# Attention in a graph network on one core: VectorE's maxima and sums interleaved, and two heads' value products moved

## What is computed

```python
q = (x @ Wq + bq).reshape(N, H, HEAD)      # N = 512, H = 8, HEAD = 64
k = (x @ Wk + bk).reshape(N, H, HEAD)
v = (x @ Wv + bv).reshape(N, H, HEAD)
scores = jnp.einsum('nhd,mhd->nhm', q, k) / np.sqrt(HEAD)
adj = jnp.zeros((N, N), jnp.float32).at[edge_index[0], edge_index[1]].set(1.0)
scores = jnp.where(adj[:, None, :] == 0, -1000000000.0, scores)
attn = jax.nn.softmax(scores, axis=1)
attn_out = jnp.einsum('nhm,mhd->nhd', attn, v).reshape(N, D_OUT)
attn_out = attn_out @ Wo + bo
```

## Time and profile before

| | us |
|---|---|
| median of 3 runs | 477.36 |
| lowest and highest run | 476.39, 477.62 |
| profiled execution, its own time | 475.42 |
| its span, first to last instruction | 473.3 |
| TensorE busy | 450.0 (95%) |
| VectorE busy | 315.1 (67%) |
| ScalarE busy | 190.5 (40%) |
| GpSimd busy | 165.7 (35%) |

### The profile page before, as it was taken

How to read it: one execution, slowest core, us unless ns; L and a number is a source line. 1 busy time by engine, 2 the same in 40 slices (tenths; PEclk the granted TensorE clock), 3 DMA queues, 4 the chain that set the end, 5 groups by cost and what they waited for, 6 DMA issues and landing times.

```text
span 473.3 us, 5934 instructions
## 1 busy us (share of the span) xinstructions
PE 450.0 (95%) x2096; PEld 327.8 (69%) x2096; DVE 315.1 (67%) x570; ACT 190.5 (40%) x265; POOL 165.7 (35%) x110
## 2 busy tenths in 40 slices
PE   7999999979899998799999999999999999999996
PEld 3456544434359886678778788888888888888765
DVE  5999868999997986958865935342262237133864
ACT  5898734555133421252632353044303342227230
POOL 4000221212233996266242444144444444344100
PEclk9999999999999999799999999999999999999999
DMA  8760000000031244004011222222220332020002
GB/s 276 190 258 1 1 2 0 24 0 0 1 111 46 89 152 156 6 16 182 3 26 64 90 89 90 89 89 112 89 90 13 117 149 77 24 89 1 0 1 89
DMA packets 22474, 34.34 MB, mean 73 GB/s; under 512 B 5680, under 2 KB 5936, under 8 KB 22448
## 3 DMA queue, kind: packets, MB, share of 16 engines
q1 hardware_dynamic: 22160, 33.85, 20.3%
q10 hardware_dynamic: 288, 0.13, 0.1%
HBM read 32.93 MB, written 1.05 MB: 72 GB/s over the span
## 4 chain that ended last, share of the span: by engine, by line
PE 70%; DVE 18%; issue 6%; ACT 2%; POOL 1%; DVEq 1%; DMA 1%; POOLq 0%
PE ps L1236 15%; PE ps L1238 15%; PE ps L1237 15%; PE ps L1298 4%; PE ps L1309 4%; PE ps L1265 3%; PE ps L1264 3%; DVE rsum L947 2%; PE ps L1386 2%; DVE stats L754 2%; PE ps L1291 2%; DVE e_sb L384 2%; DVE one_src L828 1%; PE ps L1249 1%; PE ps L1565 1%
## 5 line engine op out<-in xcount | busy, mean ns | idle before, releaser
L463 POOL TENSOR_TENSOR w_lo<-w_stage,w_hi 128x1024 fp32r<-128x1024 f32 x22 | 53.6, 2434 | 129.7 <-ACT w_hi L554 118.9
L554 ACT ACTIVATE w_hi<-w_stage 128x2048 fp32r<-128x2048 f32 x23 | 43.9, 1909 | 61.8 <-PE ps L1238 61.8
L464 POOL TENSOR_TENSOR w_lo<-w_stage,w_hi 128x1024 fp32r<-128x1024 f32 x22 | 57.3, 2604 | 0.0
L1236 PE MATMUL ps<-w_hi,hid_hi 128*128 128x512 f32 x128 | 49.9, 390 | 0.5 <-DVE hid_lo L1147 0.5
L1237 PE MATMUL ps<-w_lo,hid_hi 128*128 128x512 f32 x128 | 49.8, 389 | 0.0
L1238 PE MATMUL ps<-w_hi,hid_lo 128*128 128x512 f32 x128 | 49.8, 389 | 0.0
L1236 PE MATMUL ps<-T_hi,w_hi 128*128 128x512 f32 (+1 forms) x112 | 41.0, 366 | 0.4 <-POOL w_lo L464 0.4
L1237 PE MATMUL ps<-T_lo,w_hi 128*128 128x512 f32 (+1 forms) x112 | 40.2, 359 | 0.0
L1238 PE MATMUL ps<-T_hi,w_lo 128*128 128x512 f32 (+1 forms) x112 | 40.2, 359 | 0.0
L1145 DVE TENSOR_SCALAR tmp<-ps,bl 128x512 f32<-128x512 f32 x16 | 12.0, 749 | 39.9 <-ACT hid_hi L705 39.9
L828 DVE TENSOR_SCALAR one_src<-iota_n,edge_m,edge_w 128x256 f16 x128 | 34.1, 334 | 0.4 <-POOL edge_w L500 0.4
(11 more groups left out here) (216 smaller groups left out, 998.2 us busy)
## 6 DMA issues: line engine op xcount, KB each, us to landing
w_stage<-in_L_gnn_Wr SPq DMA_DIRECT2D x8, 1024.0 KB, 5.0
w_stage<-in_L_gnn_Wl SPq DMA_DIRECT2D x8, 1024.0 KB, 5.0
w_stage<-in_L_gnn_W SPq DMA_DIRECT2D x5, 1024.0 KB, 6.6
x_sb<-in_x SPq DMA_DIRECT2D x4, 256.0 KB, 3.7
w_q<-in_L_gnn_Wq SPq DMA_DIRECT2D x1, 1024.0 KB, 7.6
w_k<-in_L_gnn_Wk SPq DMA_DIRECT2D x1, 1024.0 KB, 10.0
w_v<-in_L_gnn_Wv SPq DMA_DIRECT2D x1, 1024.0 KB, 5.9
w_o<-in_L_gnn_Wo SPq DMA_DIRECT2D x1, 1024.0 KB, 10.3
```

Of the source, the lines that this page charges most:

```text
L463: gp.tensor_tensor(w_lo[s][:, 0:2], stage[s][:, 0:2], f32(w_hi[s][:, 0:2]), ALU.subtract)
L464: gp.tensor_tensor(w_lo[s][:, 2:4], stage[s][:, 2:4], f32(w_hi[s][:, 2:4]), ALU.subtract)\
L554: nc.scalar.activation(w_hi[u % 2][:], stage[u % 2][:], ACT.Copy).then_inc(hi_made, 1)
L1236: nc.tensor.matmul(goal, a_hi, b_hi, start=start, stop=False, **kw)
```

## The change

VectorE's helpers `maxima` and the sums are cut into single operations, `max_first`, `max_second`, `max_last`, `sum_first`, `sum_second`, `sum_last`, `inverse` and `products`, and written out in a new order in which an operation of the maxima and one of the sums take turns. Each result is now announced on a semaphore of its own (`folded`, `sum_1`, `sum_2`), and the wait stands in front of the operation that uses it. TensorE does, from step 3 on, two of the four heads of `values(i-2, 0)` ahead of `scores(i+1, 1)` and two behind. The core of the diff:

```diff
+            def max_second(i):
                 v.wait_ge(max_read, i + 1)
-                link(nc.vector.tensor_tensor(s_max[:, 0:2], s_max[:, 0:2], s_max[:, 2:4], ALU.max))
+                nc.vector.tensor_tensor(s_max[:, 0:2], s_max[:, 0:2], s_max[:, 2:4], ALU.max).then_inc(folded, 1)
...
+            def sum_first(i):
...
                 else:
                     v.wait_ge(exp_done, 2 * (i + 1))
-                    link(nc.vector.tensor_tensor(half_sum[:, 0:2], e[:, 4:6], e[:, 6:8], ALU.add))
+                    nc.vector.tensor_tensor(half_sum[:, 0:2], e[:, 4:6], e[:, 6:8], ALU.add).then_inc(sum_1, 1)
...
+            products(0)
+            max_first(2)
+            sum_first(1)
+            max_second(2)
+            sum_second(1)
+            max_last(2)
+            sum_last(1)
+            values_in(3)
+            inverse(1)
+            max_first(3)
+            sum_first(2)
+            max_second(3)
+            sum_second(2)
+            max_last(3)
+            products(1)
+            sum_last(2)
+            inverse(2)
+            sum_first(3)
+            products(2)
+            for i in range(3, STEPS):
+                more = i + 1 < STEPS
+                if more:
+                    max_first(i + 1)
+                sum_second(i)
+                if more:
+                    max_second(i + 1)
+                sum_last(i)
+                if more:
+                    max_last(i + 1)
+                inverse(i)
+                if more:
+                    sum_first(i + 1)
+                products(i)
...
-                if i >= 2:
-                    values(i - 2, 0)
+                if i == 2:
+                    values(0, 0)
+                if i >= 3:
+                    values(i - 2, 0, (0, 1))
                 if i + 1 < STEPS and i != 2:
                     scores(i + 1, 1)
+                if i >= 3:
+                    values(i - 2, 0, (2, 3))
```

More of the change, by code:

```diff
@@ L895, in _, with max_first @@
             values_in(0)
-            def maxima(i):
+            def max_first(i):
                 if i >= 1:
@@ L910, in maxima, with max_last @@
                     nc.vector.tensor_tensor(s_max[:], s_bf[:, 0:4], s_bf[:, 4:8], ALU.max).then_inc(max_read, 1)
+            def max_second(i):
                 v.wait_ge(max_read, i + 1)
-                link(nc.vector.tensor_tensor(s_max[:, 0:2], s_max[:, 0:2], s_max[:, 2:4], ALU.max))
+                nc.vector.tensor_tensor(s_max[:, 0:2], s_max[:, 0:2], s_max[:, 2:4], ALU.max).then_inc(folded, 1)
+            def max_last(i):
+                v.wait_ge(folded, i + 1)
                 if i >= 1:
@@ L915, in maxima @@
                 nc.vector.tensor_tensor(m_bf[:], s_max[:, 0], s_max[:, 1], ALU.max).then_inc(max_done, 1)
-            maxima(0)
-            values_in(1)
-            for i in range(STEPS):
+            def maxima(i):
+                max_first(i)
+                max_second(i)
+                max_last(i)
+            def sum_first(i):
                 e = e_bufs[i % E_BUFS]
-                if i == 1 or DIRECT < i < STEPS - 1:
-                    maxima(i + 1)
-                r = rsum[:, i % 2, :]
                 if i == 0:
@@ L940, in _, with sum_second @@
[L940 to L945, removed]
+                    nc.vector.tensor_tensor(half_sum[:, 0:2], e[:, 4:6], e[:, 6:8], ALU.add).then_inc(sum_1, 1)
+            def sum_second(i):
+                v.wait_ge(sum_1, i + 1)
+                if i == 0:
+                    v.wait_ge(first_half, 1)
+                if i >= DIRECT:
+                    v.wait_ge(pool_half, i - DIRECT + 1)
+                other = half_sum[:, 2:4] if i < DIRECT else pool_sum[:]
+                nc.vector.tensor_tensor(half_sum[:, 0:2], half_sum[:, 0:2], other, ALU.add).then_inc(sum_2, 1)
@@ L946, in _, with sum_last, inverse @@
+            def sum_last(i):
+                v.wait_ge(sum_2, i + 1)
+                nc.vector.tensor_tensor(rsum[:, i % 2, :], half_sum[:, 0], half_sum[:, 1], ALU.add)\
+                  .then_inc(sums_made, 1)
+            def inverse(i):
                 v.wait_ge(sums_made, i + 1)
-                nc.vector.reciprocal(r, r).then_inc(rinv_made, 1)
-                if i == 1:
-                    maxima(DIRECT + 1)
+                nc.vector.reciprocal(rsum[:, i % 2, :], rsum[:, i % 2, :]).then_inc(rinv_made, 1)
@@ L950, in _, with products @@
+            def products(i):
                 v.wait_ge(rinv_made, i + 1)
@@ L955, in _ @@
                     probabilities(nc.vector, i, slice(HEADS // 2, HEADS)).then_inc(prob_done, 1)
+            maxima(0)
+            values_in(1)
+            sum_first(0)
+            sum_second(0)
+            max_first(1)
+            sum_last(0)
+            max_second(1)
+            max_last(1)
+            values_in(2)
+            inverse(0)
+            products(0)
[31 more added lines that the diff above has]
+                products(i)
             g1_row, be1_row = wait_row(GAMMA1), wait_row(BETA1)
@@ L1395, in centre, with values @@
                 last.then_inc(centred, 1)
-            def values(i, part_no):
+            def values(i, part_no, heads=(0, 1, 2, 3)):
                 mt = i % NT
@@ L1404, in values @@
                 pe.wait_ge(prob_done, 2 * i + part_no + 1)
-                for h in range(4 * part_no, 4 * part_no + 4):
+                for h in [4 * part_no + n for n in heads]:
                     rows = slice(HD * (h % 2), HD * (h % 2 + 1))
@@ L1410, in values @@
                                             skip_group_check=True)
-                last.then_inc(pv_done, 1)
+                if heads[-1] == 3:
+                    last.then_inc(pv_done, 1)
             scores(0, 0)
```

10 lines of the change are left out of this document (3 added, 7 removed).

## The result

| | before | after |
|---|---|---|
| median of 4 runs each, side by side | 477.44 us | 480.72 us |
| lowest and highest | 476.39, 477.62 | 480.62, 481.08 |
| profiled execution, its own time | 475.42 | 480.62 |
| its span | 473.3 | 478.4 |
| last copy of the attention, att_sb, starts | 133.15 | 138.19 |

The account below looks back on a forecast made before the run. VectorE was taken to set the pace in the attention. Start 1.56, steady steps 2.0 and end 0.26 made + 3.83 us, which on the median 477.36 gave 481.2 us, range 479.4 to 483.6.

Parts of the forecast that it names:

- the new wait: VectorE's steady step: sum_first(i+1) needs exponentials usable 3.03 us after m_bf's start, so VectorE stands idle for 1.07 us.
- GpSimd's part: Steady step: GpSimd's pool_sum overlaps the start of two-input sum_first and holds it up, 0.31 us of the 8.02 us period.
- Rival B: GpSimd doesn't hold sum_first up in the steady step: period 7.71 us, time 480.3 us; chance 0.20.
- The saving of 0.12 us for each unbound pair: VectorE operations needing nothing from the one before cost 0.12 us less a pair; interleaving gives back 0.71 us a step.
- Rival A: No saving from interleaving on VectorE, each pair costs the 0.04 us of a bound one: 485.2 us; chance 0.04.
- C: Exponentials come sooner, so sum_first never waits: period 6.57 us, time 478.0; chance 0.08 together with a partly shorter chain.
- D: Faster, needing C and no loss in the start: 476.5 us; chance 0.03 for all that isn't seen.
- The start: Maxima 2 to 4 on VectorE, with sums ahead of max_last: max_last(3) 1.89 us late, max_last(4) 1.56 late.
- Three steps: Steady steps from max_last(4) to max_last(7): period 8.02 us against 7.35, 3 x 0.67 = 2.0 us added.
- The end: TensorE's output tile delays centring of step 7 (+ 8.80 from max_last(6)); products(6) end 3.83 us late, 0.26 from the end.
- Rival E: TensorE's granted clock falls to the 1.2 GHz level in the longer gaps: + 4.8 us a step; chance 0.02.
- Heads moved: TensorE's four heads split two and two: scores start 0.26 us earlier, gain nothing, cost 0.3 in the last step.

Follow-up runs that it names:

- the kernel with the write alone: Changed kernel with GpSimd's pool_sum addition replaced by a memset that reads nothing; 478.45 us, ratio 1.0038.
- The kernel with neither wait nor addition: Changed kernel with products(i) ahead of sum_first(i+1) and GpSimd's pool_sum addition replaced by a memset; 474.63 us, ratio 0.9979.
- second profile of the changed kernel: The changed kernel as it is, run once more beside the kernel before; median of all seven runs 479.12 us, ratio 1.0048.
- the turns alone: Kernel before with only maxima and sums taking turns in VectorE's loop: 479.07 us, ratio 1.0057; the same with GpSimd only writing: 477.85 us, ratio 1.0038.
- old start: Changed kernel with VectorE's order of the kernel before up to the reciprocal of step 2; 479.67 us, ratio 1.0063.
- sum ahead of the reciprocal: Changed kernel with sum_first(i+1) moved in front of inverse(i); 489.76 us in two runs, ratio 1.0287.
- heads together: Changed kernel with TensorE's order of the kernel before, four heads of values(i-2, 0) ahead of scores(i+1, 1); 479.29 us, ratio 1.0066.

## Why the prediction was right

**What bounds, and the new wait.** Right. The wait is 1.07 us in every step, forecast 1.07, and the exponentials were usable at m_bf + 3.01 (forecast + 3.03).

**GpSimd's part.** Right in kind, 0.26 us a step for a forecast 0.31: the sum lasts 0.95, not 0.98, and ends at m_bf + 3.96, not + 4.01. This is the whole error of the period, 7.96 for 8.02. Rival B, 7.71, is what the kernel with the write alone shows (7.70). Its evidence, products that overlapped an addition and lost little, was not the measure: what counts is how long the addition still runs when the other wants to start. The products of the earlier trace rows fit in: they end 2.23 us after the addition, their own 2.36 less 0.13, as the sum ends 0.55 after it, its own 0.68 less 0.13. They started just ahead of its end, so little was left to wait for.

**The saving of 0.12 us for each unbound pair.** Right: from the products on every operation starts 0.08 us before the end of the one in front. The kernel with neither wait nor addition adds it up: of the five bound pairs of the earlier trace rows four are unbound there and one has 0.02 us in place of 0.04, 7.35 - 4 x 0.12 - 0.02 = 6.85, as measured. Rival A is out, and with the wait in every step C and D too. The pair that no row showed, an unbound operation behind the reciprocal, is 1.67 start to start (92.22 to 93.89), the value taken. The prediction set the page "VectorE: DVE Perf Modes" of the Trainium skill against this, by the sentence that leaving out semaphores gains nothing. The same section also says that a next operation that isn't held starts earlier, and the rows bear that one out; it was read too narrowly.

**The start.** m_bf of step 3 at 89.36 for 89.44, of step 4 at 98.51 for 98.67: 1.40 late for 1.56, by 0.08 too much in each of two stretches.

**Three steps.** 1.8 us for 2.0: the 0.06 of GpSimd's part three times. m_bf of step 7 at 122.37 for 122.73.

**The end.** The exponentials at 123.82 for 124.20, 0.3 of it carried from m_bf of step 6; the products of step 6 end at 129.01 for 129.42, + 3.42 for + 3.83. The step "from there all moves as a whole" holds in the second profile of the changed kernel (+ 3.36 at the copy) and failed in the first (+ 5.04).

**The clock.** Here the prediction was incomplete: it put the clock's part of the tail at nothing, and where a dip came that was 1.6 us short. Rival E looked for a fall in the loop, priced it at 4.8 us a step and gave it 0.02. In the loop the clock stayed at 1.00. It fell at the tail, where the sum itself had put TensorE idle for 1.9 us, and in one of the changed kernel's two profiles. The prediction named that idle time (in its + 8.80 and products at 127.06) and didn't ask what the clock would do behind it. That the forecast, without a dip, met a median with one so well is partly luck: 3.42 us of work and 1.6 of clock in the profile stand against a median difference of 3.3, because the runs of before hold dips too: its profile has one from 194 to 204 us (0.88, 0.50, 0.50, 0.50 and 0.91 in stretches of 2 us).

**Heads moved.** Right: nothing in the loop, where the bf16 copy has time to spare, and 0.2 at the end for a forecast 0.3.

## What to carry to other kernels

Before an operation is drawn forward, count from the event that releases it: 3.0 us behind the maximum here, of which the work in between covered 1.9, and the rest is idle in an engine that sets the pace. Then look at what runs on GpSimd at the new place: a saving of 0.12 us for each pair is soon outweighed where an operation with two inputs meets an addition (0.26 to 0.97 us a step here), and an operation with one input, the reciprocal, is the place to hide it. Ask as well which wait binds next: in two of the orders the scores' bf16 copy took 0.45 and 0.56 us of a step. And where an edit leaves TensorE without work for a while, look at the granted clock behind the gap before believing another reason for a long step.

## What the runs showed of the hardware

- The meeting of VectorE and GpSimd goes both ways. GpSimd first: the VectorE operation with two inputs ended its own length, less some 0.13 us, after GpSimd's (the sum, 0.68 us alone, 0.55 after it, so it took 0.95 in the changed kernel; the products, 2.29 alone, 2.15 after it, so they took 3.05 in the turns alone). VectorE first: GpSimd's addition took 3.33 for 1.26 us and handed the wait on to VectorE's next operation (1.77 for 0.68). Beside the reciprocal nothing was lost.
- TensorE's granted clock. In four kernels TensorE had no matmul at all in a stretch of 2 us (old start, both with the turns alone, sum ahead of the reciprocal), and in the 4 us behind it the clock was 0.50 to 0.66, which cost 0.4 to 1.5 us in the step. Filling the gap with useless products took the dip away. At the tail, after the same 1.90 us of idle time, two profiles had the dip (the changed kernel with 0.10 us of work in 2, heads together with 0.25) and two had not (the changed kernel again with 0.14, the old start with 0.13); what decides between them stays open.
